# Softmax sums inverted one sequence at a time inside the attention stages, first feed loads ahead of the last group, and the second attention's start-up waits placed at the first use

## The reference, cut to what matters

```
x = x + attn_a(layernorm(x))   # 16 heads of 16, causal softmax over all keys, out projection
x = x + ffn(layernorm(x))      # gate/up 256 -> 704, silu, down; inputs and weights rounded to FP4 blocks of 16
x = x + attn_b(layernorm(x))   # 16 heads, rotary; keys: the last 128, every 64th; softmax, out projection
x = x + ffn(layernorm(x))      # the same weights
```

## Time and profile before

| | us |
|---|---|
| median of 3 runs | 3148.17 (3146.51 to 3150.44) |
| the profiled execution, its own time | 3137.59 |
| its span, first to last instruction | 3135.9 |
| busy PE / DVE / ACT / POOL, share of the span | 94% / 84% / 54% / 41% |
| mean granted TensorE clock | 0.967 of full |

### The profile page before, as it was taken

How to read it: one execution, slowest core, us unless ns; L and a number is a source line. 1 busy time by engine, 2 the same in 40 slices (tenths; PEclk the granted TensorE clock), 3 DMA queues, 4 the chain that set the end, 5 groups by cost and what they waited for, 6 DMA issues and landing times. The chain is left out here.

```text
span 3135.9 us, 105499 instructions
## 1 busy us (share of the span) xinstructions
PE 2946.0 (94%) x41228; PEld 2161.9 (69%) x41260; DVE 2625.3 (84%) x5413; ACT 1697.9 (54%) x3301; POOL 1270.7 (41%) x1572
## 2 busy tenths in 40 slices
PE   6999999999999799999996994999999969999999
PEld 4556777777777377777774653878777647777776
DVE  5778999999999499999994993777777669999997
ACT  5646787778788533333333662666656623333333
POOL 3561222112222244444432882555555624444442
PEclk9998999999999899999998996999999979999999
DMA  6682444444443222222223665455555322222221
GB/s 209 219 242 61 100 104 99 99 95 95 95 98 81 73 84 86 87 88 86 87 66 106 219 213 143 127 143 139 141 139 137 95 85 88 83 89 88 84 89 52
DMA packets 362151, 353.88 MB, mean 113 GB/s; under 512 B 79066, under 2 KB 298714, under 8 KB 361642
## 3 DMA queue, kind: packets, MB, share of 16 engines
q1 hardware_dynamic: 357162, 347.56, 40.0%
q10 hardware_dynamic: 4608, 0.79, 0.1%
HBM read 211.37 MB, written 135.27 MB: 111 GB/s over the span
## 5 line engine op out<-in xcount | busy, mean ns | idle before, releaser
L948 DVE TENSOR_REDUCE aA_nmax<-bank 128x1 f32<-128x512 f32 (+3 forms) x1216 | 715.5, 655 | 59.8 <-PE bank L1008 53.5
L990 ACT ACTIVATE aA_prob<-bank 128x512 f32<-128x512 f32 (+1 forms) x1216 | 617.0, 581 | 153.5 <-PE bank L1008 148.2
L1008 PE MATMUL bank<-aA_qk 96*32 96x512 bf16 (+17 forms) x12288 | 654.5, 317 | 13.6 <-issue 6.5
L1008 PEld LDWEIGHTS bank<-aA_qk 99*32 99x32 bf16 (+1 forms) x12288 | 408.7, 96 | 176.9 <-issue 48.3
L933 POOL TENSOR_SCALAR_AFFINE_SELECT aA_prob<-aA_prob 128x512 f32<-128x512 f32 x256 | 160.9, 634 | 663.3 <-ACT aA_prob L990 663.3
L1008 PE MATMUL bank<-aA_prob,aA_vq 128*32 128x512 f32 (+3 forms) x3072 | 357.1, 490 | 0.9 <-POOL aA_prob L933 0.9
L1498 PE MATMUL bank<-aB_qk 96*32 96x160 bf16 (+4 forms) x9344 | 309.4, 230 | 31.6 <-POOL aB_og L1321 18.5
L1498 PEld LDWEIGHTS bank<-aB_qk 96*32 96x32 bf16 (+3 forms) x9344 | 243.1, 98 | 97.9 <-issue 34.4
L1468 ACT ACTIVATE aB_prob<-bank 128x512 f32<-128x512 f32 (+1 forms) x512 | 262.3, 575 | 81.8 <-PE bank L1498 77.9
L1375 DVE TENSOR_REDUCE aB_nnear<-bank 128x3 f32<-128x480 f32 (+1 forms) x352 | 207.8, 636 | 55.7 <-PE bank L1498 50.6
L1356 POOL TENSOR_SCALAR_AFFINE_SELECT aB_prob<-aB_prob 128x512 f32<-128x512 f32 x256 | 163.4, 638 | 194.1 <-ACT aB_prob L1468 192.5
(11 more groups left out here) (212 smaller groups left out, 6195.3 us busy)
## 6 DMA issues: line engine op xcount, KB each, us to landing
aA_qk<-parts_A SPq DMA_DIRECT2D x384, 128.0 KB, 3.9
aB_qk<-parts_B SPq DMA_DIRECT2D x384, 128.0 KB, 3.3
parts_A<-pA_part SPq DMA_DIRECT2D x96, 256.0 KB, 4.8
parts_B<-pB_part SPq DMA_DIRECT2D x96, 256.0 KB, 3.1
o_A<-aA_o_sb SPq DMA_DIRECT2D x32, 512.0 KB, 3.0
o_B<-aB_o_sb SPq DMA_DIRECT2D x32, 512.0 KB, 2.9
pA_xin<-x SPq DMA_DIRECT2D x16, 512.0 KB, 4.5
v_A<-pA_vs SPq DMA_DIRECT2D x16, 512.0 KB, 4.6
```

The lines of the kernel that those rows point to most:

```text
L948: nc.vector.tensor_reduce(dst, src, AX.X, ALU.max, negate=True).then_inc(s["m_taken"], 1)
L990: nc.scalar.activation(dst, src, ACT.Exp, scale=SCALE).then_inc(s["e_taken"], 1)
L1008: return nc.tensor.matmul(out, lhsT, rhs, start=start, stop=True, skip_group_check=True)
```

## The change

1. **`invert_sums` becomes `sums(sp, n)`**, called in every turn of SP's loop in both attend stages. At n = 4, 8, ... 28 it waits until all groups so far are stored and loads `den` of the sequence just ended; at n = 7, 11, ... 31 it stores that sequence's `rden`. DVE makes the reciprocal of one sequence directly behind `turn` of group 7, 11, ... 31: six of seven come amid the attend work.
2. **Feed**: `last(sp)` no longer waits for the stores to land. That wait and the `den` load of sequence 7 stand ahead of tile 4 instead of tile 2, its reciprocal, store and the wait for it each one tile later.
3. **`early` of both stages** loads nothing at unit 15; `load_qk` of group 2 comes behind the stores of unit 15. In B `early` also loads the values of groups 0 and 1 (`load_v`).
4. **Waits of attend B at first use**: ACT's `all_stored` stands at the first `exp` of group 0, PE's `ones_set` at the first product with values, and POOL waits for `part2_ready` and `odd_ready` ahead of its memsets; the two memsets of `og` are gone. To make that safe the tiles are laid out anew: `vq`, `pgT` low, `vs`, `vt`, `pg` in the space that project B never uses; feed B's room moves with them.

```diff
+    def sums(sp, n):
+        if n >= NG and n % NG == 0:
+            for q in range(2):
+                sp.wait_ge(o_stored[q], 16 * n // 2)
+            b = n // NG - 1
             sp.dma_start(den[:, b, :], sums_of(o_dram, b)).then_inc(s["den_loaded"], 16)
+        if n >= 2 * NG - 1 and n % NG == NG - 1:
+            b = n // NG - 1
             sp.wait_ge(s["rden_ready"], b + 1)
             sp.dma_start(by_tile(rden_dram, b), den[:, b, :]).then_inc(s["rden_stored"], 16)
...
     def early(sp, unit):
-        n = unit - 13
-        if n >= 0:
-            if n == 2:
-                sp.wait_ge(done["xn_ready"], UNITS)
-                sp.wait_ge(done["xT_turned"], UNITS)
+        if unit in (13, 14):
+            n = unit - 13
             load_qk(sp, n)
             load_fixed(sp, n)
-            if n < 2:
-                sp.dma_start(qg[n][KROWS:K_GLOB, :, :],
+            sp.dma_start(qg[n][KROWS:K_GLOB, :, :],
...
+            load_v(sp, n)
     def sync(sp):
+        sp.wait_ge(done["xn_ready"], UNITS)
+        sp.wait_ge(done["xT_turned"], UNITS)
+        load_qk(sp, 2)
+        load_fixed(sp, 2)
+        load_v(sp, 2)
         sp.wait_ge(done["v_done"], UNITS)
-        for n in range(3):
-            load_v(sp, n)
+        sp.wait_ge(done["prod_ready"], UNITS * 4)
         load_qk(sp, 3)
         load_fixed(sp, 3)
         for n in range(NQ):
-            if n == NQ - 1:
-                invert_sums(sp)
-            else:
+            sums(sp, n)
+            if n < NQ - 1:
                 store_o(sp, n)
...
     def last(sp):
         store_o(sp, NQ - 1)
-        for q in range(2):
-            sp.wait_ge(o_stored[q], 16 * (NQ // 2))
...
         for kind, n, i in PLAN["dve"]:
             pieces[kind](n, i)
-        dve.wait_ge(s["den_loaded"], 16 * (BATCH - 1))
-        for b in range(BATCH - 1):
-            nc.vector.reciprocal(den[:, b, :], den[:, b, :]).then_inc(s["rden_ready"], 1)
+            if kind == "turn" and n >= 2 * NG - 1 and n % NG == NG - 1:
+                b = n // NG - 1
+                dve.wait_ge(s["den_loaded"], 16 * (b + 1))
+                nc.vector.reciprocal(den[:, b, :], den[:, b, :]).then_inc(s["rden_ready"], 1)
...
             act.wait_ge(s["e_made"], after("e", "exp", n, i))
+            if n == 0 and i == 0:
+                all_stored(act, done)
...
-        all_stored(act, done)
...
+            if n == 0 and k == 0:
+                pe.wait_ge(s["ones_set"], N_ONES)
             pe.wait_ge(s["vq_made"], n + 1)
...
-        pe.wait_ge(s["ones_set"], N_ONES)
...
                 if isinstance(k.t, int) and k.t == 2:
                     last(sp)
+                if isinstance(k.t, int) and k.t == 4:
+                    for stored in core.sems("a_o_stored"):
+                        sp.wait_ge(stored, 16 * (NQ // 2))
                     sp.dma_start(den[:, :], sums_of(o_dram, BATCH - 1)).then_inc(s["den_loaded"], 16)
```

More of the change, by code:

```diff
@@ L881, in early @@
     def early(sp, unit):
-        n = unit - 13
-        if n >= 0:
-            if n == 2:
-                sp.wait_ge(done["xn_ready"], UNITS)
-                sp.wait_ge(done["xT_turned"], UNITS)
-            load_qk(sp, n)
+        if unit in (13, 14):
+            load_qk(sp, unit - 13)
     def sync(sp):
+        sp.wait_ge(done["xn_ready"], UNITS)
+        sp.wait_ge(done["xT_turned"], UNITS)
+        load_qk(sp, 2)
         sp.wait_ge(weights.quantised["d"], 1)
@@ L1219, in attend_sparse_stage @@
     o_v = o_dram.rearrange("g p (b t) -> g b p t", t=T)
-    N_ONES = 4
+    N_ONES = 2
     def qk_uses(n):
@@ L1314, in last @@
         store_o(sp, NQ - 1)
-        for q in range(2):
-            sp.wait_ge(o_stored[q], 16 * (NQ // 2))
     def gpsimd(pool):
+        pool.wait_ge(done["part2_ready"], UNITS * 4)
+        pool.wait_ge(done["odd_ready"], UNITS)
         for r in range(2):
             nc.gpsimd.memset(vq[r][:, :, :, DH:2 * DH], 1.0).then_inc(s["ones_set"], 1)
-            nc.gpsimd.memset(og[r][:, :], 0.0).then_inc(s["ones_set"], 1)
         for r in range(2):
@@ L1819, in step @@
         def step(at):
-            if (k := at(LOAD)) and isinstance(k.t, int) and k.t == 5:
+            if (k := at(LOAD)) and isinstance(k.t, int) and k.t == 6:
                 dve.wait_ge(s["den_loaded"], 16)
@@ L2039, in build @@
                                              masks, own, kfix_d, qfix_d, gfix_d, room)
-                room = Room(nc, "fB", base, end, (130 * KB, B_FREE), (162 * KB + 512, None), (0, 32 * KB))
+                room = Room(nc, "fB", base, end, (128 * KB, B_FREE), (166 * KB, None), (0, 32 * KB))
                 feed_after = QT, {line: len(units) for line, units in SEQ.items()}
```

38 lines of the change are left out of this document (15 added, 23 removed).

## The result

Right behind the prediction the changed kernel took 3095.86 us (median of 4 executions, 3094.45 to 3098.52) and the kernel before 3147.34 (4 executions, 3142.73 to 3150.44): ratio 0.9839, 95% interval 0.9822 to 0.9856. That is 51.5 us apart. Three of the four executions of the kernel before (3146.51 to 3150.44) are the ones that the prediction counted down from.

What follows compares the result with a forecast made beforehand. PE, busy 94% of the span, was taken as the bound, with gains only at stage hand-overs. Terms -18, -6, -19 and +5 sum to -38: 3110 us for the median (3099.6 profiled), range 3097 to 3126.

Steps and rivals of the forecast that it cites:

- the level: Starting time for the sum: median 3148.2 of three runs, 10.6 above the profiled 3137.6, the same difference taken off both.
- start of attend B, -19: Hand-over from project B to attend B: ACT and PE wait less, 19 us saved, range -13 to -22.
- The delay d: Start of attend B: early value loads ahead of the stores delay `gneg` by 1.3 to 3.6 us.
- the way from ACT's start to the first `exp`: Start of attend B: 19.9 us before the change, kept for after it, putting the first `exp` at about 1925.
- the rival that I gave 14%: Three starts: shorter waits keep PE's clock up, 3 to 4 us more each, about -10, total 3100; chance 14%.
- Start of feed B, -18: Hand-over from attend B to feed B: tile 2 is ready earlier, 18 us saved, range -14 to -19.
- feed A, -6: Hand-over from attend A to feed A: only tile 2 comes earlier, 6 us saved, range -3 to -6.
- Reciprocals, +5: Attend A and B: twelve reciprocals of 0.83 us amid the work, half their time costs PE, 5 us.
- Slower: Attend stages: reciprocals between `turn` and the next group's maxima make the kernel slower than before, 3155; chance 3%.
- no effect: Changed hand-overs: first work still waits on another store or buffer, time stays at 3148; chance 2%.
- half given back: Start of attend B: late stores, `gfix` and group 2 loads cut the gain to 14 or 10, 3119; chance 18%.
- reciprocals in full: Attend stages: every reciprocal is paid, +10 or twice that, 3115 to 3124; chance 5%.

Runs made afterwards that it cites:

- `e_vlate`: Changed kernel with the values of groups 0 and 1 loaded late, behind unit 15's stores and group 2's queries and keys: 3115.7 us.

## Why the prediction was wrong, point by point

Two terms failed: the level from which the sum was counted down, and the start of attend B, -19 for a measured -24.6. Against the profiled execution, for which the prediction said 3099.6, the changed kernel's 3095.6 is 4.0 off.

- **The level: failed.** The prediction took the 10.6 us between the profiled execution and three others as a fixed offset and counted down from 3148.2. Over 56 executions the kernel before has its median at 3141.4. That is 6.8 us of the 13.9 between 3110 and the changed kernel's 3096.1. Had the same sum of -38 been taken off 3141.4, it would have said 3103. The right reading of "profiled 3137.6, runs 3146.5 to 3150.4" was a spread of over 10 us, to be put into the range. (In the comparison right behind the prediction the kernel before did come at 3147.3; there the whole miss shows as a gain of 51.5 for 38. The runs since show 39 to 44.)
- **Start of attend B, -19: too small**, measured -24.6, which is most of the other 7. ACT's moved wait and PE's wait for `pg` went as forecast; three terms were off. The delay d was taken at the middle of 1.3 to 3.6 and came out at 3.5 in the first pair of profiles (`gneg` 28.1 us behind the projection instead of 24.6) and 3.1 in the means, within the bounds; that works against the gain. The five DMAs of a value load took 5.9 us to issue, not 3.6, and the other estimate of d, near 1 us, was too low. The term that was mis-sized is the way from ACT's start to the first `exp`: taken over unchanged as 19.9 us, it was 16.0 (in the means 20.4 and 15.5). Of that 3.3 us are PE's two products at the full clock (2.00 and 1.93 us for 3.67 and 3.56). This is the rival that I gave 14%, priced at 3 to 4 us a start; it came at one of its three places. Its reason was only half right, since the clock was not kept up but rose in time for the two products. The 1 to 2 us for group 2's loads were paid (1.06 to 3.70 us over four profiles), but behind the mark, in the stretch of attend B.
- **What the early value loads are for: missed.** They were priced as a delay alone. `e_vlate` shows that ACT's moved wait would have given 3.6 of the 24.6 us without them.
- **Start of feed B, -18, and feed A, -6: right**, measured -17.3 and -6.6; PE's idle time ahead of the first projection 1.50 us where "at most 2" was said.
- **Clock in the feeds: no gain**, against the same rival: PE still waits for tile 2, and the gate product took 4.85 us for 5.06. Only the projection of tile 0 ran at the full clock in feed B, 1.10 us for 2.05, and that lies ahead of the wait.
- **Reciprocals, +5: not refuted.** The stages grew by 0.9 and 3.9, and of the latter group 2's wait is 2.1 in the mean. By the starts of DVE's instructions a reciprocal holds DVE for 0.86 us amid the stages and 0.81 in a row of seven; the 0.93 above is its record's length, which overlaps the next.
- **Slower, no effect, half given back, reciprocals in full: did not come.** PE's longest single wait for DVE's `nfar` went from 0.4 to 0.6 us.

## What to carry over

Before a time is predicted, look how far the executions at hand lie from each other and from the profiled one; the level they give is itself uncertain by that much, and a gain is better forecast as a difference. When a wait is moved to its first use, list everything else that this first use needs (here the values for `vq`): it is worth next to nothing unless that comes as early (3.6 of 24.6 us). And where PE waits at a hand-over, count the slower products behind the wait too (3.3 us here), both when it is taken away and when it is put in.

## What the runs showed of the hardware that was not expected

- A 4.8 KB load issued right behind one of 17 rows and 136 KB was in use 10.9 to 12.4 us later (12 profiles), and 6.2 us later where the 17 rows went as 16 and 1 (one profile), in the same place.
- Issuing through a second queue slowed the first: with ACT issuing fourteen loads beside them, six stores went from 4.84 to 11.18 and from 6.78 to 13.56 us of issue on SP (one profile each). With SP alone the same six took 3.90 to 8.83 us.
- One kernel on one core spreads over 18 us of 3140 from execution to execution (16.6 among 29 executions on one chip). In four profiles of the changed kernel attend A differs most, by 7.1 us.
